# Where GpSimd issues the next batch's row gathers in a two-layer transformer kernel

## The reference

```
# layer 0, feed-forward: mixture of 8 experts, top 2 per token
out = sum over e of w_e * (gelu(xf @ w1[e] + b1[e]) @ w2[e] + b2[e])
x = x + gb * out
# layer 1, attention over 64 anchors, 16 heads
attn = softmax(qk @ W_anchor.T * scale)            # per token and head
s    = sum of attn over the tokens
out  = attn @ ((attn.T @ v) / s)                   # then @ W_out.T + b_out
# layer 1, feed-forward: 128 -> 512 (gated) -> 512 -> 512 -> 128
h = silu(x @ w1) * (x @ w2); h = gelu(h @ h1); h = gelu(h @ h2); y = h @ w3
```

## Time and profile before

| | us |
|---|---|
| three runs | 889.75, 894.37, 894.45 (median 894.37) |
| profiled execution, its time | 889.55 |
| profiled execution, its span from first to last instruction | 887.8 |
| busy in that span: PE | 700.8 (79%) |
| DVE | 548.5 (62%) |
| ACT | 435.5 (49%) |
| GpSimd | 269.0 (30%) |
| mean granted clock of PE | 0.875 of full speed |

### The profile page before, as it was taken

How to read it: one execution, slowest core, us unless ns; L and a number is a source line. 1 busy time by engine, 2 the same in 40 slices (tenths; PEclk the granted TensorE clock), 3 DMA queues, 4 the chain that set the end, 5 groups by cost and what they waited for, 6 DMA issues and landing times.

```text
span 887.8 us, 9405 instructions
## 1 busy us (share of the span) xinstructions
PE 700.8 (79%) x2945; PEld 493.8 (56%) x2945; DVE 548.5 (62%) x1331; ACT 435.5 (49%) x733; POOL 269.0 (30%) x218
## 2 busy tenths in 40 slices
PE   3567545549999994079996989996899987899997
PEld 1455435538878883045554745564655565556465
DVE  4468543927667772458466668367577477596553
ACT  3355314227777772124255734265644267443475
POOL 2124776810000002624245114254134073043000
PEclk8677765569999997569998979998999998999999
DMA  5642811635777771100000000010000010000000
GB/s 199 247 154 113 315 45 42 229 112 189 233 241 250 244 254 51 33 0 0 1 21 28 13 13 1 0 31 18 24 1 1 0 44 5 25 0 1 1 1 25
DMA packets 21551, 71.17 MB, mean 80 GB/s; under 512 B 4908, under 2 KB 5172, under 8 KB 17080
## 3 DMA queue, kind: packets, MB, share of 16 engines
q1 hardware_dynamic: 17400, 62.08, 19.8%
q0 software_dynamic: 4096, 8.40, 2.9%
HBM read 47.38 MB, written 23.08 MB: 79 GB/s over the span
## 4 chain that ended last, share of the span: by engine, by line
PE 55%; POOL 15%; DVE 14%; issue 8%; ACT 4%; DMA 3%; SPq 0%; DVEq 0%; ACTq 0%; POOLq 0%
PE ps L1346 11%; PE ps L1342 8%; POOL yb L513 7%; PE ps L1350 7%; PE ps L1349 7%; PE ps L1581 6%; POOL rows_by_expert L488 6%; PE ps L1597 6%; PE ps L1348 4%; PE ps L1569 3%; DVE stats L860 2%; DVE hid L1246 2%; PE ps L1713 2%; PE ps L1389 1%; DVE ring L1262 1%
## 5 line engine op out<-in xcount | busy, mean ns | idle before, releaser
L513 POOL DMA_INDIRECT yb<-y_by_expert,ypos x64 | 64.0, 1000 | 183.4 <-DMA y_by_expert<-ysb 164.6
L1346 PE MATMUL ps<-hid,fh 128*128 128x512 f32 x256 | 105.6, 413 | 3.0 <-DVE hid L1246 2.3
L1246 DVE TENSOR_TENSOR hid<-ring,hid 128x512 fp32r<-128x512 f32 x96 | 69.4, 730 | 51.3 <-ACT hid L766 49.8
L1348 PE MATMUL ps<-hid,fh 128*128 128x512 f32 x256 | 100.7, 393 | 0.0
L554 POOL TENSOR_TENSOR misc<-misc,ring 128x1024 f32<-128x1024 f32 x28 | 65.9, 2352 | 85.4 <-DVE ring L1237 73.9
L488 POOL DMA_INDIRECT rows_by_expert<-h,pos x64 | 67.4, 1053 | 30.9 <-issue 18.1
L1346 PEld LDWEIGHTS ps<-hid,fh 128*128 128x128 f32 x256 | 48.1, 188 | 24.7 <-DVE hid L1246 11.7
L1581 PE MATMUL ps<-ring,hn 128*128 128x512 f32 x112 | 55.6, 618 | 5.3 <-DVE ring L1237 5.3
L1141 DVE TENSOR_TENSOR hid<-ring,hid 128x512 fp32r<-128x512 f32 x46 | 31.8, 692 | 41.8 <-ACT hid L574 41.8
L1597 PE MATMUL ps<-attnT,cmat 128*128 128x512 f32 x128 | 56.9, 592 | 0.0
L804 ACT ACTIVATE ring<-ps 128x1024 f32<-128x1024 f32 x32 | 32.8, 1024 | 47.7 <-PE ps L1569 47.5
(11 more groups left out here) (268 smaller groups left out, 1675.1 us busy)
## 6 DMA issues: line engine op xcount, KB each, us to landing
wbuf<-w_split SPq DMA_DIRECT2D x23, 1024.0 KB, 5.3
w_split<-parts SPq DMA_DIRECT2D x4, 2048.0 KB, 7.4
xs<-rows_by_expert SPq DMA_DIRECT2D x23, 256.0 KB, 5.3
y_by_expert<-ysb SPq DMA_DIRECT2D x23, 256.0 KB, 5.6
raw<-in_w SPq DMA_DIRECT2D x8, 512.0 KB, 7.9
ffn_raw<-in_ffn SPq DMA_DIRECT2D x1, 2816.0 KB, 14.9
rows_by_expert<-zeros SPq DMA_DIRECT2D x9, 256.0 KB, 2.0
xa<-in_x SPq DMA_DIRECT2D x4, 512.0 KB, 6.8
```

The lines of the kernel that those rows point to most:

```text
L513: gp.indirect_dma_start(yb[:, k, t, :], None, ydisp, bass.IndirectOffsetOnAxis(ypos[:, b, k, t:t + 1].bitcast(U32), 0))\
L1246: v.tensor_tensor(hid[:, s, c, 1, :], ring[:, slot, :], f(hid[:, s, c, 0, :]), ALU.subtract)\
L1346: te.matmul(out_, w(0), x(0), start=first, stop=False)
L1348: return te.matmul(out_, w(0), x(1), start=False, stop=last_)
```

## The change

The gathers of batch b+1 leave the feed-forward stage of batch b. They are issued in its attention stage: one behind each of the additions of tiles 1 to 6, and the other ten behind the addition of tile 7. The order of the gathers among themselves, their destinations, their semaphores and the wait on `dve_comb` are as before. The gathers of batch 0 stay where they were.

```diff
-            def gather(b, g):
-                if b:
-                    pool.wait_ge(*dve_comb.now(g, b - 1))
-                for t in range(g * GT, (g + 1) * GT):
-                    for k in range(TOP_K):
-                        gp.indirect_dma_start(yb[:, k, t, :], None, ydisp,
-                                              bass.IndirectOffsetOnAxis(ypos[:, b, k, t:t + 1].bitcast(U32), 0))\
-                            .then_inc(gathered[g], 16)
+            places = [(t, k) for t in ts for k in range(TOP_K)]
+
+            def gather(b, part):
+                for t, k in part:
+                    if b and (t % GT, k) == (0, 0):
+                        pool.wait_ge(*dve_comb.now(t // GT, b - 1))
+                    gp.indirect_dma_start(yb[:, k, t, :], None, ydisp,
+                                          bass.IndirectOffsetOnAxis(ypos[:, b, k, t:t + 1].bitcast(U32), 0))\
+                        .then_inc(gathered[t // GT], 16)
...
-            for g in gs2:
-                gather(0, g)
+            gather(0, places)
...
                     gp.tensor_tensor(asum, asum, ring[:, 2 * (t % 2):2 * (t % 2) + 2, :]
                                      .rearrange("p a n -> p (a n)"), ALU.add).then_inc(*pool_asum.raise_(t))
+                    if more:
+                        gather(b + 1, places[t - 1:t] if t < T - 1 else places[T - 2:])
                 rstd1("L1b", 0, b)
                 rstd1("L1b", 1, b)
                 if more:
-                    for g in gs2:
-                        gather(b + 1, g)
                     prepare(b + 1)
```

## The result

The changed kernel takes 897.68 us in the median of 17 runs (894.10 to 902.14), the kernel before 889.01 on the same chip (17 runs, 884.35 to 894.84). The ratio is 1.0089, with a 95% interval of 1.0067 to 1.0111: slower by 0.9%, where I had forecast 881 and faster. The profiled execution took 895.67, with a span of 893.8, 6.0 more than before.

The account below looks back on a forecast made before the run. PE held 55% of the chain of waits; feed-forward gathers on GpSimd (15%) delayed ACT, DVE and PE. 889.55 - 15.4 (stall) + 1.7 (sixth gather) + 2.7 (clock) = 878.6, plus 2.4: 881 us; 8 in 10 between 873 and 888.

Parts of the forecast that it names:

- the stall that goes: Feed-forward, DVE's chain to L1262: waits of 2.57, 1.77 and 0.79 us vanish, 5.13 per batch, -15.4 us in three batches.
- the 0.79 us within the pair at 610.26: Feed-forward, DVE: the pair takes 2.08 us where one with both inputs there takes 1.29; counted in the 5.13 gained.
- The clock in the feed-forward: PE still pauses some 3.45 us there, with 3.4 us at half clock behind it: 0.9 per batch, +2.7 us.
- a longer low stretch: Rival, feed-forward: 6.8 us of half clock, costing 2.6 per batch instead of 0.9; 883.7 or 886 us; chance 0.15.
- The gathers behind additions 1 to 5: Attention: each gather needs 1.25 us, at most 1.74, and fits a 3.00 us gap of GpSimd; cost nothing.
- The gather behind addition 6: Attention: held by DVE's L1237, last addition 0.75 late, PE's weight load 0.56 late; +1.7 us for three batches.
- The ten gathers behind the last addition: Attention, GpSimd: 12.5 us in all, 3.1 left before L519 of the second norm is wanted; cost nothing.
- my case on the slower side: Rival: the ten gathers delay the second norm, eating the gain from 1.64 us each; 906 us at 2.2; chance 0.03.
- The allowance of 2.4 us: Whole kernel: half the distance between two levels of the runs, added to 878.6 to give a median of 881.
- The sign on the whole: Whole kernel: chance 0.92 for faster, 0.05 for the same, 0.03 for slower.

Follow-up runs that it names:

- the modulation experiment: Changed kernel, but GpSimd's modulation of group 0 waits for DVE's combination of group 1: 885.31 us against 890.45 before (0.9936) on a fast chip, 0.9787 on a slow one.
- the four late gathers: Changed kernel with the modulation's wait, none behind addition 6, seven gathers behind addition 7, four between the L1b powers: ratios to before 0.9743, 0.9737, 0.9648 on slow chips.

## Why the prediction was wrong, point by point

**The step that failed** is in the part on the stall that goes: "So DVE finds both inputs, ends its pair at 607.25, and goes on without a wait through `combine(b+1, 1)` to L1262, as it did before between 612.34 and 616.38." Without a wait it did go on, but not as before. I moved DVE's chain forward by 5.13 us and left GpSimd's where it was in my mind. Yet the modulation follows DVE's `normalized` and moved with it, by less: `normalized` lost only 2.57 us of waiting, `combine` all of 5.13. Before, L525 (608.57 to 609.83) was over well before L1166 at 612.26; after, L526 at 607.91 and L1166 at 608.95 overlap, and L1166 takes 3.24 instead of 1.13: 2.11 of the 5.13 are lost there. The modulation takes 2.27 instead of 1.26 because it begins beside DVE's pair of L1246, and that too keeps it under L1166 for longer. Taking the overlap away brought the 4.93 back (shown by the modulation experiment). The Trainium skill has the rule, page "SBUF — State Buffer", section "Who interferes with whom": a VectorE instruction with two inputs in SBUF contends with a GpSimd instruction that reads SBUF. I had applied that section to the gathers alone. The trace agrees with it here, with the numbers just given.

The profile that I predicted from held the sign. I put the 0.79 us within the pair at 610.26 down to an input that came late. Its longer half, 1.47 instead of 0.69, had its input, and lay beside GpSimd's L527.

**The second loss in the same chain, 0.30 us,** is L520 beside DVE's pair: 1.39 instead of 1.02 to 1.05. Not forecast, same kind.

**The clock in the feed-forward.** With the chain 2 us longer PE's pause is 5.70 and not 3.45, and the half clock behind it 6.8 and not 3.4 us. The half clock starts at 613.2, 2.8 us ahead of PE's first product, so 4 us of it fall on products. Before, the same 6.8 us lay under DVE's chain. The piece up to the next L544 is only 1.34, 1.42 and 0.61 us shorter, from the 2.81 at L1262: 1.4 to 2.2 lost. My case of a longer low stretch gave 2.6 of loss for 6.8 us, and had the rest of the chain at its full 5.13; its cause (a chain that stays long) was not in it. With the modulation moved, pause and stretch came out as forecast on the fast chip, and the piece is 3.5 to 3.6 shorter, where 4.2 was forecast; that the stretch was 3.4 us there is in part luck, since the same pause had 6.8 behind it in 9 of 24 cases.

**The gathers behind additions 1 to 5** cost nothing, as forecast: 21.4 us from addition 2 to 6 in every profile.

**The gather behind addition 6** was held until DVE's L1237 had ended: 428.42, 555.90 and 685.48 in the three attentions, 1.76 to 1.78 us each (forecast "about 1.7 us long"), last addition 0.78 late (forecast 0.75), PE idle 0.36 released by L554 (forecast "about half a microsecond"). The mechanism and its size stand; the price was wrong. I wrote that PE has no pause behind it and stopped there. The short stand was followed by 3.4 us at 0.52, in which L1713 took 5.39 instead of 3.70, and such a batch lost 2.3 us, not 0.56. (In the first attention the same stand had no half clock behind it, and the batch lost 0.6.) That the stand brings the half clock was shown twice: without gathers both are gone, and with the wait filled by products the half clock is gone. In the six profiles that have this gather and an unfilled stand, 16 of the 18 stands have it behind them. It is the same kind of term that I had priced for the feed-forward and not here.

**The ten gathers behind the last addition** didn't delay the second norm: on the fast chip the chain ran past them as forecast, and my case on the slower side (each over 1.64 us) didn't occur; they took 0.95. On three of four slow-chip profiles with eleven there (L574 or L576, by the edit) ACT's step came up to 3.2 us late. So the place did hold a danger, but by another way than I priced.

**The attention's start,** +1.9 us in the table, is what I didn't forecast at all. In the first profile of before the half clock lasted 10.1, 3.4 and 3.4 us there, after 10.2 three times. Whether the change lengthens it is not settled: a second profile of the changed kernel had 6.8, 10.2 and 10.2, a third, on a slow chip, 10.2 three times, the four of before on slow chips 10.2 ten times and 6.8 and 3.4 once each, and the two of the four late gathers shown above 6.8 three times and 10.2 three times. The profile that I predicted from lay at the short end. The pause ahead of it is the jump shown above, which the change leaves alone.

**The allowance of 2.4 us** for the upper of two levels was too much for the kernel before: of its 17 runs four lie at 894.4 to 894.8, the other thirteen at 884.3 to 890.6, with a median of 889.01. It is small beside the rest.

**The sign on the whole.** Of the 15.4 us for the stall, three batches kept 8.4 at L1262 (2.81 each); 6.3 went to the combinations and 0.7 to the rest of that chain. Of the 8.4, 3.4 were left at the next L544, so 5.0 went in the stretch with the half clock, forecast 2.7. The attention's end took 5.2 where 1.7 was forecast, and its start 1.9 where nothing was. That is 7.0, 2.3, 3.5 and 1.9, together 14.7 of the 15.0 us between forecast and profile. Both steps repaired on the fast chip would be 885.3 less 6.9 (the run with the modulation's wait has the slow end in all three attentions), 878 us; that is an estimate from two experiments and was not timed as one kernel there. My cases held the gather's hold, a longer half clock and a late norm; none held an operation that grows because its neighbour moved. That is why 0.03 for slower was far too little.

## What stays open

What makes ACT stand on slow chips while gathers are in flight, and whether it is the chip at all: each slow chip served for one set of runs, so chip and hour are not separated. No run separates the transfers' data, their descriptors and the engines' own instruction supply. They are there beside runs of 16 and of 11 gathers, and absent beside ten and in the version with seven and four; that is an association over fourteen profiles, not a cause. Also open are what sets the length of a half-clock stretch, and 4 us of the modulation experiment. So the change is a loss of 0.8 to 0.9% where before takes 889 us and a gain of 1.4% on the one slow chip where it ran by itself.

## What to carry to other kernels

When a wait goes, move every engine's chain forward by its own amount, and look which operations come to lie side by side that didn't before, above all DVE with two inputs in SBUF beside GpSimd. An operation that takes longer than its like, with its inputs there, may already have such a neighbour. Give each new stand of PE two prices, its length and the half clock behind it, even where it is 0.36 us. And read more than one profile, on more than one chip, before a stretch of half clock or a stall enters a sum.

## What the runs showed of the hardware that I had not expected

- Four `scalar_tensor_tensor` of 128x128 took 3.24 us instead of 1.13 beside two GpSimd `tensor_tensor` of 128x512. The first two took 1.38 and 1.41 instead of 0.34, and each ended 0.15 us behind the GpSimd operation beside it. The first GpSimd operation had itself begun under a DVE `tensor_tensor` pair; it took 2.27 instead of 1.26.
- An indirect DMA that GpSimd began under DVE's `tensor_tensor` of 128x1024 took 1.77 us instead of 0.95 and ended 0.85 us behind it.
- A stand of PE of 0.36 us was followed, from 2.0 us behind it on (689.68 to 691.70), by 3.4 us at 0.52 of full clock in two of three attentions, although PE was busy, as the profile counts it, on both sides of it.
- PE stood 2.49 us at the change of batch ahead of products that waited for nothing, while its sequencer held a jump over the other copy of the feed-forward for 3.48 us.
- The same kernel took about 889 us in two sets of runs and about 920 on four other chips; the same program on two chips, with half clock of other lengths in the feed-forward and at the attention's start, differed by 3 us in two of three batches.
